# A gated feed-forward block whose second layer is taken as three split passes in two of its three cycles

## The reference

```python
def coupling_net(h):                       # weights 512x512, 512x256, 256x128, 128x1
    h = gelu(h @ w1 + b1)
    h = gelu(h @ w2 + b2)                  # the second layer
    h = gelu(h @ w3 + b3)
    return sigmoid(h @ w4 + b4)

gf = global_net(mean over the tokens)      # one number per batch
out = x
for _ in range(3):                         # three gating cycles
    tf = coupling_net(out)
    coupling = 0.1 + adaptive_range * (0.7 * gf + 0.3 * tf - 0.5) * 2.0
    out = out + coupling * twist(out)      # twist permutes and negates quarters of the 512 columns
```

## Time and profile before

| | |
|---|---|
| time, median of 3 runs | 1787.79 us (1784.71 to 1788.57) |
| the profiled execution, its own time | 1788.19 us |
| its span, first to last instruction | 1786.3 us |
| TensorE busy | 1755.9 us (98%) |
| VectorE busy | 1436.3 us (80%) |
| ScalarE busy | 1229.3 us (69%) |
| GpSimd busy | 654.6 us (37%) |
| mean granted clock of TensorE | 0.992 of full |

### The profile page before, as it was taken

One profiled execution on the slowest core, in us unless ns is written; L12 is line 12 of the kernel. 1 busy time (PEld: TensorE's weight loads), 2 busy tenths in 40 slices (PEclk: granted clock), 3 DMA queues, 4 the chain that ended last, 5 costly groups with the idle time before them and its releaser, 6 DMA issues. The chain is left out here.

```text
span 1786.3 us, 33819 instructions
## 1 busy us (share of the span) xinstructions
PE 1755.9 (98%) x12328; PEld 1280.2 (72%) x12328; DVE 1436.3 (80%) x2518; ACT 1229.3 (69%) x2149; POOL 654.6 (37%) x591
## 2 busy tenths in 40 slices
PE   7999998999999999999999999999999999999997
PEld 6888887777777777777777777777784674774853
DVE  5544545999999999999999999999675966857848
ACT  3232224999999999999999999999754454445435
POOL 3342342323278552477432785542334020110100
PEclk9999999999999999999999999999999999999999
DMA  7678675766367654477753685644504441330101
GB/s 265 250 247 288 231 262 160 174 167 133 115 171 196 130 140 113 122 214 142 155 143 92 164 200 124 142 96 123 187 12 135 136 117 40 110 95 0 63 1 47
DMA packets 152212, 254.60 MB, mean 143 GB/s; under 512 B 17024, under 2 KB 69504, under 8 KB 152064
## 3 DMA queue, kind: packets, MB, share of 16 engines
q1 hardware_dynamic: 101408, 157.73, 27.4%
q0 software_dynamic: 50080, 93.87, 23.6%
q10 hardware_dynamic: 576, 1.05, 0.2%
HBM read 168.44 MB, written 84.15 MB: 141 GB/s over the span
## 5 line engine op out<-in xcount | busy, mean ns | idle before, releaser
L967 DVE CUSTOM_DVE_ANT_0 a_neg<-a_sc_ps,am 128x1024 f32<-128x1024 f32 x512 | 621.0, 1213 | 1.1 <-PE a_sc_ps L820 1.1
L916 ACT ACTIVATE a_prob<-a_neg,a_row_min 128x1024 f32<-128x1024 f32 x512 | 586.6, 1146 | 7.4 <-DVE a_row_min L967 4.3
L832 PEld LDWEIGHTS a_tr_ps<-ident,a_prob 128*128 128x128 f32 x4096 | 460.6, 140 | 136.1 <-issue 100.3
L832 PE MATMUL a_tr_ps<-ident,a_prob 128*128 128x128 f32 x4096 | 546.0, 276 | 1.4 <-ACT a_probT L896 1.4
L942 DVE COPY a_probT<-a_tr_ps 128x512 f32<-128x512 f32 x512 | 353.8, 691 | 49.0 <-PE a_tr_ps L832 36.5
L896 ACT ACTIVATE a_probT<-a_tr_ps 128x512 f32<-128x512 f32 x512 | 305.6, 597 | 74.2 <-PE a_tr_ps L832 49.0
L1299 PE MATMUL f_acc<-f_u,f_w 128*128 128x512 f32 x384 | 173.2, 595 | 0.0
L716 POOL DMA_DIRECT2D a_q_st<-q_parts x144 | 79.4, 557 | 210.8 <-PE a_sc_ps L820 175.5
L853 PE MATMUL a_o_ps<-a_probT,v_first 128*32 128x256 f32 x2048 | 137.0, 385 | 0.0
L853 PE MATMUL a_o_ps<-a_probT,a_v 128*32 128x256 f32 x2048 | 136.4, 385 | 0.2 <-ACT a_probT L896 0.2
L1299 PEld LDWEIGHTS f_acc<-f_u,f_w 128*128 128x128 f32 x384 | 71.7, 190 | 89.4 <-issue 76.8
(11 more groups left out here) (210 smaller groups left out, 2948.1 us busy)
## 6 DMA issues: line engine op xcount, KB each, us to landing
a_q_st<-q_parts POOLq DMA_DIRECT2D x144, 128.0 KB, 2.9
k_first<-k_parts POOLq DMA_DIRECT2D x24, 512.0 KB, 8.0
a_k_st<-k_parts POOLq DMA_DIRECT2D x24, 512.0 KB, 7.5
a_m_raw<-mask SPq DMA_DIRECT2D x24, 512.0 KB, 4.9
a_adj_raw<-adj SPq DMA_DIRECT2D x24, 512.0 KB, 5.9
p_x_raw<-x POOLq DMA_DIRECT2D x8, 1024.0 KB, 7.7
k_parts<-p_out_hi SPq DMA_DIRECT2D x32, 256.0 KB, 2.8
k_parts<-p_out_lo SPq DMA_DIRECT2D x32, 256.0 KB, 6.0
```

What stands on the lines that cost most here:

```text
L832: last = pe.transpose(tr_ps[:, half, j * P:(j + 1) * P], prob[:, r % NPROB, t * P:(t + 1) * P], ident[:])
L916: act.activation(prob[:, r % NPROB, :], neg[:, r % 2, :], ACT.Exp, scale=-1.0, bias=row_min[:, r % 2:r % 2 + 1], accum_out=row_sum[:, r // ...
L967: dve.tensor_tensor_reduce(out=neg[:, r % 2, :], in0=sc_ps[:, r % 2, :], in1=am[:, 2 * qb + qt, :], scale=-1.0, scalar=3.4e38, op0=ALU.add ...
```

## The change

In cycles n = 0 and 1 (the constant `SPLIT`) layer 2 is no longer one f32 product but a `three_pass` of split operands; the third cycle stays as it was. For that:

- ScalarE computes the GELU behind layer 1 twice in these cycles: into `u_hi[j]` in the F32R format, then in place into `u[j]` as before;
- VectorE subtracts, `u_lo = u - u_hi`, in `split_u`, four instructions a turn, over the place of `u`; for cycle 1 this stands behind the whole `mix` of its turn, for cycle 0 among the `add_shared` of half 1;
- `w2` is split once a batch, into `w2_hi` by ScalarE and `w2_lo` by VectorE, since their place is used for other data in between;
- `u_hi[0]` lies over the second buffer of x rows and `u_hi[1]`, `w2_hi` and `w2_lo` lie over the attention tiles of half 0. So the load of x for half 1 waits for layer 2 of turn 2, and the load of attention for half 0 for layer 2 of turn 3; GpSimd now issues half 1 ahead of half 0.

```diff
+    SPLIT = 2
...
+        u_hi_at = [sb.offset, SB_K0]
         x_rows = [staged("f_x_rows0", [P, TT, E]), sb("f_x_rows1", [P, TT, E])]
+        u_hi = [nc.alloc_sbuf_tensor_at(f"f_u_hi{j}", [P, ET, CH], F32R, offset=u_hi_at[j]) for j in range(NJ)]
+        w2_hi = nc.alloc_sbuf_tensor_at("f_w2_hi", [P, ET, F2], F32R, offset=SB_K0 + 8192)
+        w2_lo = nc.alloc_sbuf_tensor_at("f_w2_lo", [P, ET, F2], F32R, offset=SB_K0 + 12288)
...
+        u_at = [sb.offset + 4 * ET * CH * j for j in range(NJ)]
         u = [sb(f"f_u{j}", [P, ET, CH]) for j in range(NJ)]
+        u_lo = [nc.alloc_sbuf_tensor_at(f"f_u_lo{j}", [P, ET, CH], F32R, offset=u_at[j]) for j in range(NJ)]
...
                     for j in range(NJ):
-                        if not first:
-                            sp.wait_ge(x1_ready, TT * (NJ * b + j + 1))
+                        if j == 1:
+                            sp.wait_ge(z2_ready, 2 * turn(b, SPLIT - 1, 0) + 2)
+                        elif not first:
+                            sp.wait_ge(x1_ready, TT * (NJ * b + 1))
                         load_x(b + 1, j)
...
-            def load_attention(b, j):
-
-                wait(pool, product_ready, 4 * ET * (NJ * (b - 1) + j + 1) if b else 0)
+            def load_attention(b, j, part):
+
+                if j == 0:
+                    pool.wait_ge(z2_ready, 2 * turn(b - 1, SPLIT - 1, 1) + 2)
+                else:
+                    pool.wait_ge(product_ready, 4 * ET * (NJ * (b - 1) + j + 1))
...
                 if more:
-                    load_attention(b + 1, 0)
-                    load_attention(b + 1, 1)
+                    for j in (1, 0):
+                        for part in range(2):
+                            load_attention(b + 1, j, part)
...
                 for t in tiles:
+                    if n < SPLIT:
+                        pe.wait_ge(w2_lo_ready, b + 1)
+                        pe.wait_ge(u_lo_ready, ET * turn_split(b, n, j) + t + 1)
+                        for m in range(2):
+                            ms = slice(m * P, (m + 1) * P)
+                            last = three_pass(pe, acc[:, 2 * j + m, :], w2_hi[:, t, ms], w2_lo[:, t, ms], u_hi[j][:, t, :], u_lo[j][:, t, :],
+                                              t == 0, t == ET - 1)
+                            if t == ET - 1:
+                                last.then_inc(z2_ready, 1)
+                        continue
                     pe.wait_ge(h1_ready, ET * k + t + 1)
...
                 act.wait_ge(shared_read, 4 * (ET * (NJ * b + j) + m) + 4)
+                act.activation(u_hi[j][:, m, :], A[j][:, m, :], ACT.Gelu, bias=small.b1[:, m:m + 1])
                 act.activation(u[j][:, m, :], A[j][:, m, :], ACT.Gelu, bias=small.b1[:, m:m + 1]).then_inc(h1_ready, 1)
+
+            def split_w2(b):
+                act.wait_ge(product_ready, 4 * ET * (NJ * b + 1))
+                if b == 0:
+                    act.wait_ge(w_loaded, 32)
+                act.activation(w2_hi[:], w2[:], ACT.Copy).then_inc(w2_hi_ready, 1)
...
                 act.wait_ge(u_ready, ET * k + m + 1)
+                if n < SPLIT:
+                    act.activation(u_hi[j][:, m, :], u[j][:, m, :], ACT.Gelu, bias=small.b1[:, m:m + 1])
                 act.activation(u[j][:, m, :], u[j][:, m, :], ACT.Gelu, bias=small.b1[:, m:m + 1]).then_inc(h1_ready, 1)
...
                 last.then_inc(g1_ready, 1)
+                split_w2(b)
                 read_own(b, 1, 1)
...
+            def split_w2(b):
+                dve.wait_ge(w2_hi_ready, b + 1)
+                dve.tensor_tensor(w2_lo[:], w2[:], w2_hi[:].bitcast(F32), ALU.subtract).then_inc(w2_lo_ready, 1)
+
+            def split_u(b, n, j):
+                for m in range(ET):
+                    dve.wait_ge(h1_ready, ET * turn(b, n, j) + m + 1)
+                    dve.tensor_tensor(u_lo[j][:, m, :], u[j][:, m, :], u_hi[j][:, m, :].bitcast(F32), ALU.subtract).then_inc(u_lo_ready, 1)
...
                 add_shared(b, 1, 0)
+                split_w2(b)
                 add_shared(b, 1, 1)
                 add_shared(b, 1, 2)
+                split_u(b, 0, 0)
                 add_shared(b, 1, 3)
+                split_u(b, 0, 1)
...
                         coefficients(b, n, j)
                         mix(b, n + 1, j)
+                        if n + 1 < SPLIT:
+                            split_u(b, n + 1, j)
```

More of the change, by code:

```diff
@@ L1102, in ffn_phase @@
         h1_ready = sem("f_h1_ready")
+        u_lo_ready = sem("f_u_lo_ready")
+        w2_hi_ready = sem("f_w2_hi_ready")
+        w2_lo_ready = sem("f_w2_lo_ready")
         z2_ready = sem("f_z2_ready")
@@ L1125, in turn, with turn_split @@
             return (CYCLES * b + n) * NJ + j
+        def turn_split(b, n, j):
+            return (SPLIT * b + n) * NJ + j
         def coef_steps(b, n, j):
@@ L1180, in _ @@
         def _(pool):
-            def load_attention(b, j):
-                wait(pool, product_ready, 4 * ET * (NJ * (b - 1) + j + 1) if b else 0)
+            def load_attention(b, j, part):
[3 more added lines that the diff above has]
+                    pool.wait_ge(product_ready, 4 * ET * (NJ * (b - 1) + j + 1))
                 pool.wait_ge(weighted.stored, 32 * 2 * GPB * (b + 1))
-                for part, tile in enumerate((X_hi[j], X_lo[j])):
-                    src = weighted.parts[part, :, b * S + j * CH:b * S + (j + 1) * CH].rearrange("(t p) s -> p t s", p=P)
-                    pool.dma_start(tile[:], src).then_inc(X_loaded[j], 16)
+                src = weighted.parts[part, :, b * S + j * CH:b * S + (j + 1) * CH].rearrange("(t p) s -> p t s", p=P)
+                pool.dma_start((X_hi, X_lo)[part][j][:], src).then_inc(X_loaded[j], 16)
             pool.memset(minus_half[:], -0.5).then_inc(filled, 1)
```

## The result

| | before | after |
|---|---|---|
| time, median | 1788.18 us (1784.71 to 1790.43, 4 runs) | 1821.36 us (1817.58 to 1822.0, 4 runs) |
| ratio, 95% interval | | 1.0189 (1.0173 to 1.0205) |
| span of the profiled execution | 1786.3 us | 1819.3 us |
| TensorE, VectorE, ScalarE busy in it | 1755.9, 1436.3, 1229.3 us | 1750.8, 1485.2, 1269.7 us |

The change makes the kernel slower by 33 us. The forecast was 1810, the range 1795 to 1828. In the kernel after, the numbers of the lines move: the f32 product of layer 2 is L1328, layers 3 and 4 are L1336 and L1344, `split_u` is L1624, the mix L1650 to L1660, the GELUs of cycle 1 L1462 (high part) and L1463, the gate L1476. L164 to L166 are the split passes.

What follows compares the result with a forecast made beforehand. TensorE's work and a slackless chain through the other engines were taken to bound the turns. Four batches at +4.0 (+16), +4 for batch 0 and +1.7 for the clock made +22: forecast 1810 us, range 1795 to 1828.

Steps and rivals of the forecast that it cites:

- the clock: One more fall of TensorE's clock to 1.2 GHz, from the new stalls: +1.7 us, bounds 0 and 14.
- the sum per batch: Each batch: -5.7 products, +0.3 pass changes, +9.1 stalls and activation wait, +0.3 first layer, giving +4.0 us; four times +16.
- The bound and the chain: Gating turns: TensorE busy throughout, but the chain through gate, coefficients, mix and GELU to the third cycle has no slack.
- the five places named: TensorE stalls: tile 0 of turns 2, 3, 4 (0.85, 2.35, 2.3 us), tile 2 of turns 2 and 3 (1.5 each).
- What is removed: Layer 2, 4 turns of 8 products a batch: 0.177 us saved each, 1.42 a turn, 5.7 a batch, 22.7 in all.
- 0.17 for the wait for layer 2's first activation: Split turns: wait for layer 2's first activation grows from 0.1 to 0.27 us, 0.6 to 0.7 a batch.
- the 0.3 for the pair: First layer: ScalarE's extra GELU ahead of pair_hi delays pair_lo and TensorE, +0.3 us a batch, bounds 0 and 0.6.
- The 0.3 a batch for changes from f32 to split passes: First split pass after f32 has its successor 0.32 us behind, not 0.23; two a turn, bounds 0 and 0.7.
- sign of 62 to 63 us for the turns: Changed profile: gating stretches of 62 to 63 us instead of 59; shorter than 59 would make the prediction wrong.
- The first layer: Extra GELU ahead of pair_hi costs +0.3 us a batch; w2 split fits in idle time and loads cost nothing.
- Batch 0: GpSimd's last attention splits slow VectorE's two-SBUF-operand instructions on the chains of turns 2 and 3: +4 us, bounds 0 and 8.
- the clock goes with the stalls: Rival, chance 0.08: each stall over 2 us brings 3.4 us at 1.2 GHz, +6 to +12, so 1816 to 1822 us.

Runs made afterwards that it cites:

- e1: Changed kernel with only the first cycle split (SPLIT = 1): 1782.12 us, ratio 0.9966 to the kernel before.
- e2: Changed kernel without the eight cycle 1 subtractions a batch, second GELU straight into u_lo, output not the reference's: 1780.93 us, ratio 0.9963 to the kernel before.
- e3: Changed kernel with ScalarE's GELU pairs of tiles 2 and 3 of cycle 1 ahead of the gate: 1796.31 us, ratio 1.0046 to the kernel before.
- e4: Changed kernel with unread products added on TensorE ahead of its waits in the turns: 1810.1 us, ratio 1.0126 to the kernel before.
- e7: First-cycle-only split with GpSimd held in batch 0, plus half 0's tile 2 GELU pair moved behind half 1's pair-sum split: 1777.72 us, ratio 0.9953 to before.
- e5: Changed kernel with the eight cycle 1 subtractions a batch moved from VectorE to GpSimd: 1821.85 us, ratio 1.0198 to the kernel before.

## Why the prediction was right, point by point

The direction, the stalls and 22 of the 33 us were forecast. Of the other 11 the clock is 7 (9.0 for 1.7), the sum per batch 2.4 and the later begin of the phase 1.2. The forecast's own range had 14 us on the upper side, so it holds the measured time, though by a term for the clock that was too small by a factor of five.

- **The bound and the chain.** Right. The sum put the chain through gate, coefficients, mix and GELU beside TensorE's own work and found no slack where it leads to cycle 2; five stalls followed at the five places named, by starts each within some 0.1 us of its size. e1, e2 and e3 show that the reason was the named one, the place of `split_u` and of the GELUs that it waits for.
- **What is removed.** Right in size. In e1, batch 2, a turn with all its products split is 1.19 us shorter than before: from layer 4 to layer 3 5.24 against 6.10, from layer 3 to layer 4 3.21 against 3.54. That is the forecast's 1.42 less its 0.17 for the wait for layer 2's first activation. Two such turns less the 0.3 for the pair give e1's 2.1; its expectation of 2.4 had left the activation out. The 0.3 a batch for changes from f32 to split passes was read wrongly: the 0.32 in the earlier trace rows stands behind the 16 one-column products, and in e1 a split pass behind layers 3 and 4 costs nothing more. A first pass behind a stall does have its successor 0.31 behind (1502.91 and 1503.22), which costs 0.4 a batch in another place.
- **The sum per batch.** +4.0 forecast, +4.6 measured in e4 free of the clock (batches of 126.1 against 121.5). The parts as measured are -4.8 (four turns at 1.19), +8.7 for the stalls, +0.3 for the pair and +0.4 behind the stalls. Four times: 18.4 instead of 16. The forecast's sign of 62 to 63 us for the turns came out as 64.1 in e4, batch 1, free of the clock, against 59.9 before; part of the difference is that its 59 had been cut 0.7 short.
- **The first layer.** Right in place and size: TensorE's wait for pair_lo rose from 0.3 us in batch 0 to 1.0 and from none to 0.3 in each of the others, and e7 takes 0.33 a batch away by moving that GELU. The split of w2 and the loads cost nothing, as said.
- **Batch 0.** +4 forecast, some 4.2 measured in the trace after: 2.14 us of wait at layer 3 of turn 0, 1.0 more at tile 0 of turn 2 than in the other batches (1.76 for 0.79), and 1.1 more from layer 4 of turn 1 to tile 0 of turn 3 (12.17 for 11.06). In e4 4.8 are left over (11.1 - 4.6 - 1.65, a stretch at 1.2 GHz having cost 1.65 before). The place was only half right: the forecast named the chains of turns 2 and 3, and the largest piece was on the subtractions of the first layer, 6.20 for 2.48, which end in the wait at turn 0. By the Trainium skill's "GPSIMD Engine Reference", Key points, which has VectorE instructions with two SBUF inputs contend with GpSimd, these subtractions are exposed; the trace agrees, and so do e5's products and sums.
- **The clock.** This is the term that was mis-sized: +1.7 for one more stretch at 1.2 GHz (bounds 0 and 14). There were seven more in the profiled execution. In batches 1 to 3 they account for 4.9, 3.0 and 0.9 us above 126.1, less 1.6 and 1.6 before: 5.6. The one of batch 3 is partly hidden, since the next stall shrinks from 1.42 to 0.72. In batch 0 they account for 3.4: of its three stretches the one in turn 2, behind the stall of 2.04, lies ahead of tile 0 of turn 3, which comes by VectorE's chain and is waited for anyway, so it costs nothing. That is 9.0 us; the mean clocks put it at 12 with the hidden parts counted, and e4 gives 11 back. The rival "the clock goes with the stalls", to which I gave 0.08, was the better account, and not by its number alone: it had a stretch behind each stall over 2 us, and seven of the nine waits over 2 us have one behind them, and none of the shorter ones in turns has. The Trainium skill, "TensorE: Matmul & The Clock Gate", section on HAM oscillation, describes a kernel whose waits for transfers of some 3 to 5 us drop the clock again and again. The pauses here that have a stretch behind them are shorter, 2.04 to 2.18 us, so that description does not cover them.
- **The ledger.** 18.4 (four batches) + 4.2 (batch 0 beside GpSimd) + 9.0 (clock) + 1.2 (phase begun later) = 32.8, of 33.0 between the spans. Why the phase began later is open; it is no work of the change.

## What to carry to other kernels

A saving on the busy engine is worth only what the chain round the other engines lets through: write that chain down from one trace, with its starts, before the edit; if it has no slack, each microsecond taken from the busy engine is a microsecond of stall. A wait inside a hand-written list costs by what stands behind it, not by its own work: the same eight subtractions were worth 40 us in one place, and four GELUs moved past one tanh gave 25 us back. Where two recurring steps can take a cheaper form and only one has slack, change that one alone: here the first cycle, 1777.7 us with the two small moves.

## What the runs showed of the hardware

- A stall costs TensorE more than its length when the clock falls behind it: four instructions of layer 2 that took 1.98 us took 3.68. Filling the pauses with products that nobody reads took a kernel from 1821.36 to 1810.1 us, more work in less time.
- When it falls stays open. In the changed kernel all seven stretches at 1.2 GHz in turns began within 1.5 us behind a stall of over 2 us; but two such stalls brought none, e5's of 2.5 us brought none in batches 1 to 3 of one execution, and the kernel before had two stretches without a stall. The count differs between executions of one kernel, so one trace is no measure of it: among four runs after, the one with the mean clock at 0.988 took 1817.58 us and the two at 0.985 took 1822.0 and 1821.61. Part of the spread of this kernel's times goes with that.
- VectorE and GpSimd slow each other when both work on SBUF: 0.68 us became 1.75 to 1.78 for a product and a sum of VectorE, 1.49 for a one-input instruction of 0.42, and two GpSimd subtractions of 1.27 each took 3.44.
